# A fused layer norm, autocorrelation and gated FFN on one core: the first group's loads, copies and low parts are put in another order, and the last tile is finished in halves

## Chip, cores, metric
One core of one Trainium2 chip. The metric is the device time of one execution in microseconds (us). TensorE is called PE, VectorE DVE, ScalarE ACT, GpSimd POOL, and the queue of SyncE, which issues most transfers, SP.

## The reference
x is 4096 tokens by 1024. Each token is normalised to xn. A gated feed-forward layer is applied to xn, its weights tiled four times over and with rank-2 additions; its silu is g. s is an autocorrelation of xn: the six strongest lags of each row, softmaxed, weight six rolled copies of xn. The result is x + s*g.

```python
xn = _layernorm(x, axis=-1)
s = _L0_attn_ref(xn)
g = _silu(_L0_ffn_ref(xn, w1q, a1, b1, w3q, a3, b3, w2q, a2, b2))
x = x + s * g
```

The kernel computes on the chip a flag that says whether in every row lag 0 leads by so much that s is xn itself. With these inputs it does, and only the short branch (`dve.Else`) runs.

## The kernel before
The 4096 tokens are worked in 8 groups (`i`) of 512 tokens, each of 4 tiles (`q`) of 128. The quarters of xn are summed first, so that the weights need not be tiled. In a group PE runs:

- **the up stage**, 22 "pairs" (`p`) of hidden columns: `up(i, p)` makes 6 matmuls into a bank of `gb` and 6 into one of `ub` (f16 high and low parts, three products). Every odd pair begins with `lora`, four matmuls of 32 rows that add the rank-2 part from `zst` and `bst` and close the pair before too. ACT's `gate` then writes silu to `sil`, DVE's `product` makes `h`, and `add_chunk` sums four pairs into `acc`, whose high and low parts are `hf_h` and `hf_l`. `bank_free` keeps pair p behind the product of pair p - 3. After p = 5, 9, 13 and 17 comes `z2(i, n)`, eight matmuls of `h` with `a2st`.
- **the down stage**, `down(i, q)`: 34 matmuls of a tile with `w2_h` and `w2_l` into two banks. ACT writes their silu to `gg`, DVE makes `ob` in `multiply` and `add_input`, and SP stores it. The last piece of tile 0 waits for `z2_read`, that is DVE's `z2_stack`. `z_across` ahead of tile 3 waits for `zs`, which DVE's `z_split` writes.

Meanwhile DVE and POOL prepare the next group: `stats` (DVE), `spread` (POOL, small ones), `normalise` (ACT, writes `xn`), `project` (DVE, the 16 dot products of xn with the rows of a1 and a3, tile `junk`), `differences` and `sums` (POOL), `ft_load` and `xt_load` (transposing transfers).

**The first group** has all that is done once beside it. The weights w1 and w3 come in four column blocks (pairs from 0, 4, 10, 16). A block is bounded (`w_bound`, ACT, and `scale_sum` and `w_scale`), scaled and rounded (`w_high`, ACT) and its low part is made (`w_low`, DVE); PE waits for `wl_done` at the first pair of a block. b1 and b3 (tile `raw_b`, ten small transfers) are split by `b_cast` (ACT) and `b_step` (DVE) and scaled by `b_scale` (ACT); PE's `lora` waits for `b_done` at p = 1, 5, 11 and 17. POOL folds tiles 0 and 1, spreads, runs `raw_differences` for four tiles, and copies `a2st` in three pieces, for which the first `z2` waits. The high parts of w2 are ACT's, its six low parts (`w2_low`) POOL's.

The order on each engine is the order of the code; tables of pair numbers say at which pair a step stands. Every wait is a semaphore written out by hand.

```python
if p % 4 == 1 and 4 < p < NP_ - 1:
    z2(i, p // 4 - 1)
...
if n == 0:
    if i:
        pe.wait_ge(z2_read, i)
    else:
        pe.wait_ge(a2_done, 3)
```

Of the kernel before, what the change touches and what calls it, by code (L numbers as in the profile page):

```python
# [95 lines left out]
def build(nc, d):  # L96
# [1284 lines left out]
```

## Time and profile before

| | |
|---|---|
| median of 3 runs | 884.25 us (883.89 to 884.58) |
| the profiled execution | 883.97 us, its span 882.2 us |
| PE busy | 840.8 us (95%) |
| DVE busy | 637.7 us (72%) |
| ACT, POOL busy | 299.7 and 314.1 us |
| first matmul of the up stage of groups 0, 1, 2 | 28.10, 161.88, 263.84 us |
| last matmul starts | 874.93 us |

Times in the trace are from the span's start. A timeline row reads: start, duration, engine, line, operation, tiles, number; in brackets how long the engine had been idle and what ended that. Successive instructions of an engine overlap by a few hundredths of a microsecond, so the distance between two starts is what one costs. Nearly all elementwise operations of ACT are recorded under one line, L550; they are told apart by their tiles.

### The profile page before, as it was taken

Reading aid. Unit: us, or ns where it says so; the run is one execution under the profiler, and the core shown is the slowest. Engines: PE = TensorE matmul, PEld = TensorE weight load, DVE = VectorE, ACT = ScalarE, POOL = GpSimd, SP = SyncE. Lnnn points to the kernel's source line nnn. Section 1 sums busy time; section 2 is a strip of 40 time slices with the busy share of each in tenths; the row PEclk is TensorE's granted clock in tenths of the full one; section 3 lists DMA queues with packets and bytes.
Section 4 is the critical chain, followed back from the end, with each engine's and each line's share of the span. In section 5 each row is a group of like instructions: output and inputs, shape, how many; then the busy total and the mean of one; then the engine's idle time right before and its main releaser. Section 6 shows DMA issues by size and latency. Waiting matters only on the chain.

```text
span 882.2 us, 11146 instructions
## 1 busy us (share of the span) xinstructions
PE 840.8 (95%) x4078; PEld 436.1 (49%) x4078; DVE 637.7 (72%) x979; ACT 299.7 (34%) x448; POOL 314.1 (36%) x405
## 2 busy tenths in 40 slices
PE   5889696999999999999999999999999999999996
PEld 4333255534573346634484436743475345844465
DVE  6878987579767886678866797578866788644534
ACT  4766232332323323233322333233333333122231
POOL 6944754245404344045513444043431465000000
PEclk9899799999999999999999999999999999999999
DMA  9851003411232112501144113321135111320003
GB/s 303 266 169 36 6 25 96 173 31 32 53 126 97 36 30 55 188 28 37 30 116 154 37 31 54 120 96 36 30 55 195 27 32 20 112 96 1 1 2 143
DMA packets 51401, 70.03 MB, mean 79 GB/s; under 512 B 34961, under 2 KB 36849, under 8 KB 51073
## 3 DMA queue, kind: packets, MB, share of 16 engines
q1 hardware_dynamic: 49584, 68.46, 25.2%
q10 hardware_dynamic: 1744, 0.72, 0.3%
q8 instruction: 32, 0.52, 0.3%
q14 instruction: 41, 0.33, 0.1%
HBM read 44.52 MB, written 16.78 MB: 69 GB/s over the span
## 4 chain that ended last, share of the span: by engine, by line
PE 86%; DVE 7%; DVEq 2%; issue 2%; DMA 1%; ACT 1%; SPq 0%; POOL 0%; ACTq 0%
PE g L1123 25%; PE u L1123 23%; PE zb L1213 6%; PE g L1236 5%; PE u L1236 5%; PE u L1243 4%; PE u L1245 4%; PE g L1243 4%; PE g L1245 4%; PE g L1141 3%; DVE junk L769 2%; DMA xf<-in_x 1%; DVEq L830 1%; DVE w_l L989 1%; PE mb L1177 1%
## 5 line engine op out<-in xcount | busy, mean ns | idle before, releaser
L550 ACT ACTIVATE sil<-g,winv 128x512 f32<-128x512 f32 (+1 forms) x176 | 120.2, 684 | 275.3 <-PE g L1141 234.5
L1123 PE MATMUL u<-xt,w_h 128*128 128x512 f16 x672 | 201.4, 382 | 11.2 <-DVE w_l L989 11.2
L1123 PE MATMUL g<-xt,w_h 128*128 128x512 f16 x672 | 203.6, 385 | 1.1 <-DVE w_l L989 0.7
L814 DVE SCALAR_TENSOR_TENSOR h<-u,winv,sil 128x512 f32<-128x512 f32 x168 | 125.6, 748 | 96.6 <-ACT sil L550 82.6
L769 DVE CUSTOM_DVE_ANT_0 junk<-xn,abc 128x1024 bf16<-128x1024 f32 x112 | 159.1, 1421 | 6.7 <-issue 2.4
L438 POOL TENSOR_TENSOR ve<-mv,three 128x1 f32<-128x1 f32 x32 | 7.7, 240 | 355.7 <-DVE mv L751 355.7
L1123 PE MATMUL g<-xt,w_l 128*128 128x512 f16 x336 | 128.6, 383 | 0.0
L1123 PE MATMUL u<-xt,w_l 128*128 128x512 f16 x336 | 128.1, 381 | 0.0
L1123 PEld LDWEIGHTS u<-xt,w_h 128*128 128x128 f16 x672 | 65.9, 98 | 92.7 <-DVE w_l L989 12.7
L1123 PEld LDWEIGHTS g<-xt,w_h 128*128 128x128 f16 x672 | 57.5, 98 | 89.8 <-issue 33.3
L948 DVE SCALAR_TENSOR_TENSOR ob<-xr,c_mean,gg 128x1024 f32<-128x1024 f32 x32 | 41.1, 1284 | 76.9 <-ACT gg L550 52.5
L1236 PE MATMUL g<-w_h,hf_h 128*128 128x512 f32 x192 | 79.9, 416 | 1.4 <-issue 1.0
L1236 PE MATMUL u<-w_h,hf_h 128*128 128x512 f32 x192 | 76.4, 398 | 0.0
L550 ACT ACTIVATE gg<-g 128x512 f32<-128x512 f32 x32 | 19.2, 599 | 158.9 <-PE g L1239 83.8
L1243 PE MATMUL u<-w_l,hf_h 128*128 128x512 f32 x160 | 63.7, 398 | 0.0
L1245 PE MATMUL u<-w_h,hf_l 128*128 128x512 f32 x160 | 63.5, 397 | 0.0
L1243 PE MATMUL g<-w_l,hf_h 128*128 128x512 f32 x160 | 63.2, 395 | 0.0
L1245 PE MATMUL g<-w_h,hf_l 128*128 128x512 f32 x160 | 63.2, 395 | 0.0
L826 DVE TENSOR_TENSOR acc<-acc,h 128x512 f32<-128x512 f32 x80 | 61.7, 771 | 0.0
L1213 PE MATMUL zb<-h,a2st 128*6 128x512 f32 (+1 forms) x352 | 57.5, 593 | 0.0
L1123 PEld LDWEIGHTS g<-xt,w_l 128*128 128x128 f16 x336 | 33.2, 99 | 40.6 <-issue 1.7
L477 POOL TENSOR_TENSOR yh<-xn 128x512 f32<-128x512 f32 x28 | 36.8, 1316 | 45.9 <-ACT xn L550 45.9
(180 smaller groups left out, 1192.3 us busy)
## 6 DMA issues: line engine op xcount, KB each, us to landing
xr<-in_x SPq DMA_DIRECT2D x32, 512.0 KB, 4.6
out_x<-ob SPq DMA_DIRECT2D x32, 512.0 KB, 2.9
xf<-in_x SPq DMA_DIRECT2D x30, 512.0 KB, 3.6
raw_w<-in_w2t SPq DMA_DIRECT2D x1, 2560.0 KB
abc<-in_a SPq DMA_DIRECT2D x1, 2048.0 KB, 10.6
raw_w<-in_w1t SPq DMA_DIRECT2D x2, 768.0 KB, 13.4
raw_w<-in_w3t SPq DMA_DIRECT2D x2, 768.0 KB, 14.7
raw_w<-in_w1t SPq DMA_DIRECT2D x1, 704.0 KB, 15.6
```

What stands on the lines that cost most here:

```text
L477: tt(yh[:], x[:, 0:HALF], x[:, HALF:L], ALU.subtract).then_inc(diff_done, 1)
L550: return nc.scalar.activation(out, in_, f, **kw)
L769: nc.vector.tensor_tensor_reduce(junk[:], xn[:], abc[:, r, :], 1.0, 0.0, ALU.mult, ALU.add, zt[:, q, r:r + 1]).then_inc(z_done, 1)
L814: stt(out=h[0:n, p % NH, :], in0=up, scalar=winv[0:n, 3 * block_of(p) + 1:3 * block_of(p) + 2], in1=sil[0:n, p % 2, :], op0=ALU.mult, op1= ...
L826: o = tt(acc[0:rows, b, :], a, h[0:rows, p % NH, :], ALU.add)
L948: stt(out=o[:], in0=x[:], scalar=c_mean[:, q:q + 1], in1=gg[:], op0=ALU.subtract, op1=ALU.mult)
L1123: o = mm(bank[:], a, x, start=opens and t == 0, stop=closes and t == len(terms) - 1)
L1141: o = mm((gb, ub)[s % 2][k % 3][:], bst[32 * s:32 * s + 32, p // 2, :], zst[32 * s:32 * s + 32, :], start=s >= 2 and not first, stop=s < 2 ...
L1213: o = mm(zb[c:c + 6, :], a2st[0:rows, p, :], h[0:rows, p % NH, :], start=n == 0, stop=p + 4 >= NP_)
L1236: mm(bank[:], hf_h[:, n, t], w2_h[:, n, c:c + 512], start=n == 0, stop=False)
L1243: mm(bank[:], hf_h[:, n, t], w2_l[:, n, c:c + 512], start=False, stop=False)
L1245: mm(bank[:], hf_l[:, n, t], w2_h[:, n, c:c + 512], start=False, stop=False)
```

## The change
- **Loads.** `low` and b's ten transfers are issued by SP behind the four tiles of x, no longer by ACT ahead of its work; `sel` moves behind weight block 1, `abc` ahead of the two next tiles of x.
- **ACT.** A small silu at the very start brings the table in. `w_high(0, 0)` stands ahead of the copies to `xt`, `w_high(1, 0)` ahead of the first gate; b is cast in halves of 5 and 6 pairs of pairs; `b_scale(1)` stands at p = 2, not 3. Bounds and high parts of blocks 2 and 3 stand one or two pairs earlier.
- **DVE.** `w_low(0, 0, *)` stands ahead of `xt_low` and `zc`, low parts of blocks 2 and 3 earlier; six `w2_low` come over from POOL and stand behind the up stage; stats and projections of the first group get other pairs.
- **POOL.** `raw_differences` wait until block 0's four low parts are made (`wl_done`). The fourth stands behind `spread(1, 0)`, and `a2st` behind both.
- **PE.** The spread of z (`mb<-zc,sel`) stands behind the first six matmuls of the up stage; the first group's down stage runs the products with `w2_h` of tiles 0 and 1 first and those with `w2_l` behind.
- **First group's output.** ACT makes rs*g + 1 and adds the mean, DVE is left with one pass a tile.
- **Last tile.** Bank g is finished ahead of bank u, and silu, multiply, add and store run in halves of 512 columns.

```diff
-        STATS_AT = [(2, 8, 14, 19)] + [(1, 7, 13, 19)] * (NG - 1)
-        NORM_AT = [(3, 9, 15)] + [(2, 8, 14, 20)] * (NG - 1)
-        Z_AT = [{(4 if i == 0 else 3) + 6 * q + r: (q, r) for q in range(3) for r in range(4)} for i in range(NG)]
+        STATS_AT = [(3, 11, 17, 19)] + [(1, 7, 13, 19)] * (NG - 1)
+        NORM_AT = [(4, 12, 18)] + [(2, 8, 14, 20)] * (NG - 1)
+        Z_AT = [{p: (n // 4, n % 4) for n, p in enumerate((5, 8, 9, 10, 13, 14, 15, 16, 18, 19, 20, 21))}]
+        Z_AT += [{3 + 6 * q + r: (q, r) for q in range(3) for r in range(4)}] * (NG - 1)
...
-        BOUND_AT = {3: ((2, 0),), 4: ((2, 1),), 5: ((3, 0), (3, 1))}
-        HIGH_AT = {1: ((1, 0), (1, 1)), 6: ((2, 0), (2, 1)), 10: ((3, 0),), 11: ((3, 1),)}
+        BOUND_AT = {2: ((2, 0),), 3: ((2, 1), (3, 0)), 4: ((3, 1),)}
+        HIGH_AT = {1: ((1, 1),), 5: ((2, 0),), 6: ((2, 1),), 8: ((3, 0),), 9: ((3, 1),)}
...
-            for q in FIRST_DIFF:
+            pool.wait_ge(wl_done, 4)
+            for q in FIRST_DIFF[:3]:
                 raw_differences(q)
             pool.wait_ge(zst_done, 1)
-            pool.wait_ge(ab_done, 12)
+            pool.wait_ge(ab_done, 9)
             nc.gpsimd.memset(hf_l[64:P, HN, :].bitcast(F32), 0.0).then_inc(zeroed, 1)
             pool.wait_ge(zeroed, 11)
+            spread(1, 0)
+            raw_differences(FIRST_DIFF[3])
             pool.wait_ge(c_loaded, 16 * 3)
...
             def down(i, q):
-                if i or q:
+                if i == 0 and q:
+                    act.wait_ge(first_mult, q)
+                elif i or q:
                     act.wait_ge(final_done, at_tile(i, q - 1))
...
+                if i == 0:
+                    act.wait_ge(dn_read, 2 * q + 2)
+                    A(gg[:], gg[:], scale=c_rs[:, q:q + 1], bias=1.0).then_inc(plus_done, 1)
+
+            def first_mean(q):
+                act.wait_ge(first_mult, q + 1)
+                A(ob[q % 2][:], ob[q % 2][:], bias=c_mean[:, q:q + 1]).then_inc(final_done, 1)
...
+                if i == 0:
+                    for n in range(1, 3):
+                        w2_low(n)
...
+            def last_output(half):
+                i, q, c = NG - 1, 3, slice(HALF * half, HALF * half + HALF)
...
+                dve.wait_ge(dn_read, at_tile(i, q, 2, half + 1))
+                stt(out=o, in0=x, scalar=c_mean[:, q:q + 1], in1=gg[:, c], op0=ALU.subtract, op1=ALU.mult)
+                drain()
+                stt(out=o, in0=o, scalar=c_rs[:, q:q + 1], in1=x, op0=ALU.mult, op1=ALU.add).then_inc(half_final, 1)
```

Three places as the engines' own orders show them. POOL, from the fourth raw difference (tile `xr_68`) to the first instructions for group 1. Before:

```order
L464 TENSOR_TENSOR yh<-xr_68 128x512 [waits ab_done]
L466 TENSOR_SCALAR yh<-yh,rs 128x512 [waits raw_diff]
L468 TENSOR_TENSOR hl<-yh 128x255 [waits diff_done]
L469 TENSOR_TENSOR hl<-yh 128x255
L470 CAST hl<-yh 128x2
L525 MEMSET hf_l 64x512 [waits ab_done,zst_done]
L529 COPY a2st<-raw_a_116 128x22x2 [waits c_loaded,zeroed]
L529 COPY a2st<-raw_a_116 128x22x2 x2
L438 TENSOR_TENSOR ve<-mv,three 128x1 [waits stats_done]
```

And now:

```order
L540 MEMSET hf_l 64x512 [waits ab_done,zst_done]
L458 TENSOR_TENSOR ve<-mv,three 128x1 [waits stats_done,zeroed]
L459 TENSOR_TENSOR nm<-mv,three 128x1
L461 TENSOR_TENSOR rs<-ve,three 128x1 [waits dev_done]
L463 TENSOR_TENSOR nm<-nm,rs 128x1 [waits dev_done]
L484 TENSOR_TENSOR yh<-xr_68 128x512 [waits ab_done]
L486 TENSOR_SCALAR yh<-yh,rs 128x512 [waits raw_diff]
L488 TENSOR_TENSOR hl<-yh 128x255 [waits diff_done]
L489 TENSOR_TENSOR hl<-yh 128x255
L490 CAST hl<-yh 128x2
L546 COPY a2st<-raw_a_116 128x22x2 [waits c_loaded]
L546 COPY a2st<-raw_a_116 128x22x2 x2
```

The copies to `a2st` now stand behind an instruction that waits for DVE's first `stats` of group 1 (`stats_done`), and behind the fourth difference.

DVE, from the last product of the first group to the first projection of tile 3. Before:

```order
L814 SCALAR_TENSOR_TENSOR h<-g,winv,sil 64x512 [waits z2_done,sil_done]
L847 TENSOR_TENSOR hf_l<-acc,hf_h 128x512 [waits hfh_done]
L835 TENSOR_TENSOR half_a<-half_a,h 64x512 [waits shift_done,zeroed]
L838 TENSOR_TENSOR acc<-half_b,h 32x512 [waits hfl_done,shift_done]
L841 TENSOR_TENSOR acc<-half_b,half_a 32x512 [waits half_done,shift_done]
L847 TENSOR_TENSOR hf_h<-acc,hf_h 64x512 [waits hfh_done]
L1002 SCALAR_TENSOR_TENSOR w_l<-b_hi,low,raw_b_136 64x1024 [waits b2h_done,w2h_done]
L852 SCALAR_TENSOR_TENSOR z2f<-zb,zq 64x512 [waits zq_done]
```

And now:

```order
L830 SCALAR_TENSOR_TENSOR h<-g,winv,sil 64x512 [waits z2_done,sil_done]
L785 ISA junk,zt<-xn,abc 128x1024 [waits z_done]
L785 ISA zt 128x1
L866 TENSOR_TENSOR hf_l<-acc,hf_h 128x512 [waits hfh_done]
L1062 TENSOR_TENSOR w_l<-raw_w_138,w_h 128x1024 [waits w2h_done,zeroed]
L851 TENSOR_TENSOR half_a<-half_a,h 64x512 [waits shift_done]
L854 TENSOR_TENSOR acc<-half_b,h 32x512 [waits hfl_done,shift_done]
L1062 TENSOR_TENSOR w_l<-raw_w_138,w_h 128x1024 [waits w2h_done] x2
L860 TENSOR_TENSOR acc<-half_b,half_a 32x512 [waits half_done,shift_done]
L1062 TENSOR_TENSOR w_l<-raw_w_138,w_h 128x1024 [waits w2h_done]
L866 TENSOR_TENSOR hf_h<-acc,hf_h 64x512 [waits hfh_done]
```

The six low parts of w2 (two more follow) and one projection stand between the last product and `z2f`, which PE's last piece of tile 0 needs.

ACT, from the copy to `bst` for block 0 to the gate of pair 3. Before:

```order
L550 ACTIVATE bst<-bst,wscl 128x256 [waits wscl_done,b_rest_done]
L550 ACTIVATE b_part<-raw_b 128x1152
L550 ACT_TABLE_LOAD
L550 ACTIVATE sil<-g,winv 128x512 [waits g_ready] x2
L550 ACTIVATE w_h<-raw_w_133,wscl 128x2x768 [waits wscl_done] x2
L550 ACTIVATE sil<-g,winv 128x512 [waits mult_done,g_ready]
L550 ACTIVATE b_part<-raw_b 128x1152 [waits b_rest_done]
L550 ACTIVATE sil<-g,winv 128x512 [waits mult_done,g_ready]
L550 ACTIVATE bst<-bst,wscl 128x384 [waits wscl_done,b_rest_done]
```

And now:

```order
L559 ACTIVATE bst<-bst,wscl 128x256 [waits wscl_done,b_rest_done]
L559 ACTIVATE w_h<-raw_w_133,wscl 128x2x768 [waits wscl_done]
L559 ACTIVATE sil<-g,winv 128x512 [waits g_ready] x2
L559 ACTIVATE w_h<-raw_w_133,wscl 128x2x768 [waits wscl_done]
L559 ACTIVATE sil<-g,winv 128x512 [waits mult_done,g_ready]
L559 ACTIVATE bst<-bst,wscl 128x384 [waits wscl_done,b_rest_done]
```

The copy to `bst` for block 1 (128x384), for which PE's pair 5 waits, stands behind the gate of pair 2 with no cast ahead of it.

## Rows read from the trace of the kernel before

**Rows 1.** Windows of the span: part of group 0, then the whole of group 1.

```profile
core 0: us, PE busy (x) PEld busy (x) DVE busy (x) ACT busy (x) POOL busy (x), PEclk, DMA share, GB/s
63.66:122.20 58.54, 48.27 (x238) 19.54 (x235) 51.94 (x76) 25.42 (x38) 30.84 (x32) 0.91 0.09 25
161.88:263.84 101.96, 101.96 (x500) 52.87 (x499) 77.46 (x121) 32.59 (x49) 36.60 (x48) 1.00 0.23 73
```

**Rows 2.** Waits (us, times, longest) of PE in group 0, of DVE from 63.66 to 122.20.

```profile
PE u L1123 <- DVE w_l L989: 11.2, 3, 7.6
DVE h L814 <- ACT sil L550: 5.6, 4, 2.9
```

**Rows 3.** The head: DMA queues of 0 to 60 us, then PE's timeline.

```profile
q10 hardware_dynamic: 1744, 0.72, 4.9%
...
16.22 0.69 PE L1252 MATMUL g<-ident,xf 128*128 128x128 f32 x2 [2.05 <-DMA xf<-in_x]
28.10 1.01 PE L1123 MATMUL g<-xt,w_h 128*128 128x512 f16 x2 [0.65 <-DVE w_l L989]
49.63 0.58 PE L1141 MATMUL g<-zst,bst 32*128 32x512 bf16 x1 [3.48 <-ACT bst L550]
54.11 1.04 PE L1213 MATMUL zb<-h,a2st 128*6 128x512 f32 x8
```

**Rows 4.** Timeline of DVE in the head: low parts of blocks 0 and 1.

```profile
25.24 4.51 DVE L989 SCALAR_TENSOR_TENSOR w_l<-raw_w,wscl,w_h 128x512 f16<-128x512 f32 x4
42.68 1.95 DVE L989 SCALAR_TENSOR_TENSOR w_l<-raw_w,wscl,w_h 128x768 f16<-128x768 f32 x2
```

**Rows 5.** Timeline of POOL: the fourth difference's first and last, copies, spread.

```profile
36.33 1.27 POOL L464 TENSOR_TENSOR yh<-xr 128x512 f32<-128x512 f32 x1
...
41.87 0.19 POOL L470 CAST hl<-yh 128x2 f16<-128x2 f32 x1
42.77 2.10 POOL L529 COPY a2st<-raw_a 128x44 f32<-128x44 f32 x3
46.19 0.19 POOL L438 TENSOR_TENSOR ve<-mv,three 128x1 f32<-128x1 f32 x1 [1.32 <-DVE mv L751]
...
47.13 0.27 POOL L443 TENSOR_TENSOR nm<-nm,rs 128x1 f32<-128x1 f32 x1
```

**Rows 6.** Timelines of DVE and POOL, 81 to 109 us.

```profile
81.28 0.88 DVE L989 SCALAR_TENSOR_TENSOR w_l<-raw_w,wscl,w_h 128x640 f16<-128x640 f32 x1
89.79 2.98 DVE L989 SCALAR_TENSOR_TENSOR w_l<-raw_w,wscl,w_h 128x640 f16<-128x640 f32 x1
92.69 3.35 DVE L769 CUSTOM_DVE_ANT_0 junk<-xn,abc 128x1024 bf16<-128x1024 f32 x1
104.37 1.54 DVE L826 TENSOR_TENSOR acc<-acc,h 128x512 f32<-128x512 f32 x1
108.18 1.21 DVE L769 CUSTOM_DVE_ANT_0 junk<-xn,abc 128x1024 bf16<-128x1024 f32 x1
89.74 5.23 POOL L500 TENSOR_TENSOR w_l<-raw_w,w_h 128x1024 fp32r<-128x1024 f32 x2
```

**Rows 7.** Timelines of DVE and PE behind the up stage, 122 to 153 us.

```profile
124.30 2.86 DVE L835 TENSOR_TENSOR half_a<-half_a,h 64x512 f32<-64x512 f32 x1
130.65 0.68 DVE L841 TENSOR_TENSOR acc<-half_b,half_a 32x512 f32<-32x512 f32 x1 [0.70 <-ACT half_b L550]
132.75 1.28 DVE L1002 SCALAR_TENSOR_TENSOR w_l<-b_hi,low,raw_b 64x1024 fp32r<-64x1024 f32 x1
152.04 1.11 PE L1199 MATMUL mb<-ident,zs 128*128 128x128 f32 x4 [5.60 <-DVE zs L787]
```

**Rows 8.** Timelines of ACT, DVE and SP at the end.

```profile
875.68 0.59 ACT L550 ACTIVATE gg<-u 128x512 f32<-128x512 f32 x1
877.72 1.29 DVE L953 SCALAR_TENSOR_TENSOR ob<-ob,c_rs,xr 128x1024 f32<-128x1024 f32 x1
871.38 8.00 SPq L372 DMA_DIRECT2D out_x<-ob  x2
```

More of the change, by code:

```diff
@@ L370, in store @@
             def store(i, q):
+                if i == NG - 1 and q == 3:
+                    for half in range(2):
+                        c = slice(HALF * half, HALF * half + HALF)
+                        sp.wait_ge(half_final, half + 1)
+                        sp.dma_start(out_d[i * 4 + q][:, c], ob[q % 2][:, c]).then_inc(stored[q % 2], 16)
+                    return
                 sp.wait_ge(final_done, at_tile(i, q))
@@ L531, in _ @@
                 for q in range(4):
-                    if i == 0 and q == 2:
-                        w2_low(0)
-                        w2_low(1)
                     if i + 1 < NG:
-                        spread(i + 1, q)
-                    if i == 0 and q == 2:
-                        w2_low(2)
-                    if i == 0 and q == 3:
-                        for n in range(3, HN + 1):
-                            w2_low(n)
-                    if i + 1 < NG:
+                        if i or q:
+                            spread(i + 1, q)
                         differences(i + 1, q)
@@ L668, in b2_high @@
                 A(b2_hi[64:P, :], raw_b2[64:P, :], ACT.Copy).then_inc(b2h_done, 1)
[L670 to L678 removed]
+            act.wait_ge(zeroed, 4)
+            A(w_sq[:, 0, 0:4], three[:], ACT.Silu).then_inc(table_done, 1)
+            act.wait_ge(table_done, 1)
             w_bound(0, 0)
@@ L702, in _ @@
             b_scale(0)
-            b_cast(1, 0)
+            w_high(1, 0)
             for i in range(NG):
@@ L1038, in _ @@
             x_copy(3)
-            b_step(0, 0)
+            w_low(0, 0, 0)
+            w_low(0, 0, 1)
             xt_low(0)
@@ L1044, in _ @@
             tt(zc[:], zb[:], rsb[:], ALU.mult).then_inc(zc_done, 1)
-            for m in range(2):
-                for k in range(2):
-                    w_low(0, m, k)
-            b_step(0, 1)
+            w_low(0, 1, 0)
+            w_low(0, 1, 1)
+            b_step(0, 0)
             dve.wait_ge(z0_part, 1)
@@ L1223, in down @@
                         pe.wait_ge(dn_read, at_tile(i, 1, 2, 2))
+                if i == NG - 1 and q == 3:
+                    for bank, c in banks:
+                        for n in range(HN):
+                            mm(bank[:], hf_h[:, n, t], w2_h[:, n, c:c + 512], start=n == 0, stop=False)
+                            mm(bank[:], hf_h[:, n, t], w2_l[:, n, c:c + 512], start=False, stop=False)
+                            mm(bank[:], hf_l[:, n, t], w2_h[:, n, c:c + 512], start=False, stop=False)
+                        mm(bank[:], hf_h[:, HN, t], w2_h[:, HN, c:c + 512], start=False, stop=False)
+                        mm(bank[:], hf_l[:, HN, t], w2_l[:, HN, c:c + 512], start=False, stop=True).then_inc(dn_ready, 1)
+                    return
                 for n in ns:
@@ L1276, in z0, with z0_spread @@
                     o.then_inc(z0_ready, 1)
+            def z0_spread():
+                pe.wait_ge(zc_done, 1)
+                pe.wait_ge(sel_loaded, 16)
+                mm(mb[:], sel[:], zc[:], start=True, stop=True).then_inc(z0_ready, 1)
             pe.wait_ge(a_cent, 1)
```

199 lines of the change are left out of this document (142 added, 57 removed).

## The prediction, made before the changed kernel was run
> **What bounds the kernel now.** I read the windows first. Group 1 takes 101.96 us in which PE is busy for 101.96 at the full granted clock, and the groups behind it repeat that [rows 1]. The change leaves them alone, up to the last tile; there is nothing for it to win there. Group 0 runs from 28.1 to 161.88 us [rows 1, 3], 133.8 us, so 31.8 more than its 101.96 of work. With the head ahead of it and the tail behind the last matmul these are the only places where the change acts. PE's waits come next: in group 0 it waits 11.2 us for low parts of w1 and w3 by DVE [rows 2] and 5.6 for `zs`, again DVE's [rows 7]; another 3.5 goes to b's block 1 at pair 5, at 49.63 us [rows 3]. So DVE, or what it waits for, sets group 0. Last I read the engines' timelines at these stalls, to see what each would be late for next.
>
> **The head.** The fourth tile of x lets PE go on at 16.22 us [rows 3]. The queue q10 is b's loads: 4.9% of 16 engines over 60 us, 2.9 us of all of them, which now come behind. I take the 2.9 whole; it is between 0 (they only filled gaps) and about 4. Behind it, DVE's four low parts of block 0 took 4.51 us, 1.13 each, while POOL made differences; block 1's took 0.97 each at 768 columns with POOL elsewhere, 0.65 for 512 [rows 4]. Holding POOL thus saves 1.0 on the two ahead of PE, and `zc`, now behind them, 0.6 by its neighbours. The first matmul of the up stage comes at 28.1 - 2.9 - 1.0 - 0.6 = 23.6 us. The early table load costs nothing: ACT has no input yet. The eleven issues cost SP some 6 us, but in that time the queue works off x and block 0; what moves back (`sel`, blocks 2 and 3) is needed only from 26 us on.
>
> **Pairs 0 to 5.** Part of the 4.5 us goes back: z's spread, its two parts and `zst` now come behind the first six matmuls, and the first gate behind a `w_high` of 1.5 us. Placing each instruction by its duration before, block 1's last low part ends at 42.4 us, against 44.6 (42.68 + 1.95 [rows 4]). The larger step is `b_scale(1)`: it comes with pair 2, near 39 us, so pair 5 starts at 43.7, not at 49.63. With pair 5 and the two scale sums PE is through at 47.3 us, 6.8 ahead of 54.11, where `z2(0, 0)` started [rows 3].
>
> **A wait that replaces the one removed.** `z2(0, 0)` needs `a2st`. Before, POOL had copied it by 44.87 (42.77 + 2.10), long ahead [rows 5]. Now the copies stand behind `spread(1, 0)`, which waits for DVE's first stats of group 1, moved to pair 3 (end 45.2 by my placing), and behind the fourth difference. So: 45.2, spread 1.2 (46.19 to 47.40), difference 5.7 (36.33 to 42.06), copies 2.1 [rows 5] = 54.2, with handovers 54.4. The first three differences, held to 25.4, end near 42 and don't decide. PE stalls 7.1 us, from 47.3 to 54.4: **all that head and pairs 0 to 5 win is gone there.** The difference may cost 5.0 (POOL alone) to 6.8 (the slowest of each kind of its instructions). Behind such a stall PE runs at the lower level, 1.2 GHz, for a while: the mean granted clock of 0.91 over 58.54 us [rows 1] is some 10.5 us at half speed, and PE waited for only 7.6 of them [rows 2], so 3 us of work ran slowly. With 3 to 4 us here I take a loss of 1.9; `z2` ends at 56.3 and pair 6 starts 1.2 us later than before. What is queued behind the waiting PE waits too: ACT and DVE finish pair 5 and then have nothing until `g_ready` of pair 6.
>
> **Pairs 6 to 21: DVE.** From product 7 to product 21 DVE needed 58.54 us [rows 1], 5.6 of them waits for `sil` [rows 2], so 52.9 of work. POOL's low parts of w2 stood in its way there: one low part took 2.98 instead of 0.88, a projection 3.35 instead of 1.21, a sum 1.54 instead of about 0.7 [rows 6], 5.1 in all, and just ahead of PE's 7.6 us wait. Away with them: 47.8. One projection more (1.2), a `b_step` of about 1.0, and less two of block 2's low parts, which come one pair earlier (1.95): 48.1. Product 6 starts at 60.8 (pair 6, partly at the lower level, then `lora` and gate); pair 6's own work is 3.9, and 0.7 is waited at pair 10. Product 21 ends at 60.8 + 3.9 + 48.1 + 0.7 = 113.5, before at 122.2: 8.7 won. Block 3's low parts are there by 86, before PE's pair 16 at 88: its 7.6 wait goes. What is late next is DVE itself, whose products PE trails by `bank_free`.
>
> Here a rule can be weighed. By the row, POOL's 5.23 us of two low parts [rows 6] cost DVE 4.2. The Trainium skill, Perfetto Trace Analysis, Optimizing Scalar/DVE Operations, says that GpSimd and VectorE share an SBUF read port, so that moving work between the two might not help. By that rule this stretch would win nothing; by the rows it wins 5.1 here and pays below.
>
> **From the last product to `zs`.** This took 152.0 - 122.2 = 29.8 us. Added: six `w2_low` at 1.28, the price of DVE's own 1024-column pass at 132.75 [rows 7], 7.7, and a projection, 1.2. Removed: three operations that POOL's low parts stretched, one of them from 0.68 to 2.86 [rows 7], together 5.8; the 0.70 wait ahead of `acc` [rows 7], filled by two low parts; one pass over the tile, 1.4 with its drain; 0.4 that DVE waited for `xn`. The 1.7 that POOL's tile 3 costs stays. Sum 30.4, `zs` at 143.9. Down stage: `z2_read` near 130, and PE, with 18 matmuls of tiles 0 and 1 and 34 of tile 2 left, comes to `z_across` near 143, so the 5.6 wait [rows 7] shrinks to under 1. The later first gate of group 1 (ACT adds 1.2 four times over) has some 2 us to spare before PE's pair 3. Group 1 started 9.84 us behind `z_across` (152.04 [rows 7] to 161.88), 1.3 of it from the lower clock, which falls away: 143.9 + 8.5 = 152.4, **9.5 us earlier**.
>
> **The tail.** Bank g is done 4 us earlier; bank u's silu starts with the last matmul, not 0.5 behind it (875.68 [rows 8]). Multiply and add of 1.29 [rows 8] become 0.68 each, 1.2 less. The last store runs from 879.38 (871.38 + 8.00 [rows 8]) to the end at 882.2; half of it saves between 0 and 0.65, I take 0.4. **2.1 us.**
>
> **Sum.** 883.97 - 9.5 - 2.1 = **872.4 us**, against the profiled execution, which lies 0.3 below the median of 884.25. 0.2% of that, 1.8 us, is what a measurement can tell.
>
> **Rivals.**
> - *The `a2st` wait is short or absent* (stats earlier, differences quicker): then DVE's 7 us without work go, and it reaches product 21 some 6 us earlier: 866. Against it: the order of POOL's instructions. 8%.
> - *Collisions come back.* POOL's tile 3, brought forward, now meets the low parts of w2, and its differences meet DVE in pairs 10 to 18. Two to three hits of 2.2 us, as at 124.30 [rows 7]: 877 to 879. For it: DVE has no slack. 21%.
> - *DVE is freer than that*, the held differences leave it alone and it keeps to PE's pace: 3 to 5 us better, 868. 15%.
> - *The moved work is worth what it costs*, group 0 stays as it was, only the tail wins: 883.97 - 2.1 = 881.9. This is the port rule, as in the Trainium skill's page. 3%.
> - *Slower.* DVE was not late because of POOL's low parts, so only additions remain: 7.7 for six passes in the chain to `zs`, 1.2 for pair 6's later start, less the tail: 883.97 + 7.7 + 1.2 - 2.1 = 890.8. It decides if the relief above (5.1 and 5.8 us) comes to less than 6.8 us. Against it: the stretched operations [rows 6, 7]. 5%.
>
> The forecast's own case has 48% and runs from 869 to 876 (head 0 to 4 is absorbed by the `a2st` wait; difference 5.0 to 6.8; store 0 to 0.65; 2 us for my placing of DVE). The range takes in the faster cases and most of the collisions: 865.5 to 878.5. Faster by over 0.2%: 0.93; within: 0.02; slower: 0.05.
>
> **What would show it.** Right: first matmul of the up stage near 23.6; `z2(0, 0)` waiting about 7 us for POOL's `a2st` and starting near 54.4; no wait at pair 5 or 16; product 21 at 113; `zs` at 144; group 1 at 152; groups at 101.96. Wrong: no wait at `z2(0, 0)`; low parts on DVE well over 1.28 us; group 1 starting outside 149 to 158; a tail from last matmul to end that is not about 5 us.

## The result, and the profile after

| | before | changed |
|---|---|---|
| median | 884.07 us (883.21 to 884.58, 4 runs) | 875.16 us (874.59 to 876.60, 4 runs) |
| ratio | | 0.990, 95% interval 0.9885 to 0.9916 |
| profiled execution | 883.97 us, span 882.2 | 875.03 us, span 873.0 |
| first up matmul of groups 0, 1, 2 | 28.10, 161.88, 263.84 us | 23.00, 154.34, 256.30 us |
| from the last matmul's start to the end | 7.27 us | 5.48 us |

The change is faster by 8.9 us (1%), where 11.6 were forecast (883.97 to 872.4). By the two spans it is 9.2: group 1 starts 7.5 us earlier (forecast 9.5) and again takes 101.96 us [rows 1]; the remaining 1.7 is the tail (forecast 2.1).

Four of PE's waits up to group 1 (us in total, times, longest), where 11.2 us for low parts stood before [rows 2]:

```profile
PE zb L1295 <- POOL a2st L546: 6.5, 1, 6.5
...
PE g L1325 <- DVE hf_l L874: 4.3, 1, 4.3
PE zb L1295 <- DVE h L830: 2.8, 1, 2.8
...
PE u L1203 <- DVE w_l L1049: 2.2, 1, 2.2
```

The forecast's new wait is the longest, and there is none at pair 5 or at pair 16, as forecast. The wait for `hf_l` is the one for `z2_read`: `z2_stack` writes that piece of `hf_l`. PE's timeline at the points of [rows 3, 7] and at group 1's start:

```profile
13.69 0.69 PE L1370 MATMUL g<-ident,xf 128*128 128x128 f32 x2 [2.20 <-DMA xf<-in_x]
...
23.00 0.59 PE L1203 MATMUL g<-xt,w_h 128*128 128x512 f16 x2 [2.74 <-DVE xt L1085]
...
54.15 1.89 PE L1295 MATMUL zb<-h,a2st 128*6 128x512 f32 x8 [6.52 <-POOL a2st L546]
...
131.54 0.77 PE L1325 MATMUL g<-w_h,hf_h 128*128 128x512 f32 x1 [4.35 <-DVE hf_l L874]
132.11 0.63 PE L1325 MATMUL u<-w_h,hf_h 128*128 128x512 f32 x1
132.53 0.63 PE L1327 MATMUL g<-w_l,hf_l 128*128 128x512 f32 x1
...
136.87 0.39 PE L1318 MATMUL u<-w_l,hf_h 128*128 128x512 f32 x1
137.10 0.40 PE L1325 MATMUL g<-w_h,hf_h 128*128 128x512 f32 x1
...
145.97 0.60 PE L1281 MATMUL mb<-ident,zs 128*128 128x128 f32 x4
...
154.34 0.61 PE L1203 MATMUL g<-xt,w_h 128*128 128x512 f16 x2
```

x's fourth tile lands 2.5 us earlier, the first up matmul comes 5.1 earlier, and all of it is gone at 54.15, where `z2(0, 0)` starts as late as before [rows 3]. `z_across`, which had waited 5.60 us for `zs` [rows 7], waits for nothing at 145.97. The rows of 132.11 and 132.53 are new: successive matmuls there start 0.43 us apart; from 136.87 on they start 0.23 apart.

DVE's timeline, and then POOL's, at the same places:

```profile
45.46 0.21 DVE L767 BATCH_NORM_AGGREGATE mv<-bn 128x2 f32<-128x12 f32 x1
...
60.76 0.75 DVE L830 SCALAR_TENSOR_TENSOR h<-u,winv,sil 128x512 f32<-128x512 f32 x1 [7.84 <-ACT sil L559]
...
102.99 1.23 DVE L785 CUSTOM_DVE_ANT_0 junk<-xn,abc 128x1024 bf16<-128x1024 f32 x1 [1.35 <-ACT xn L559]
...
113.79 0.75 DVE L830 SCALAR_TENSOR_TENSOR h<-g,winv,sil 64x512 f32<-64x512 f32 x1
...
123.60 3.45 DVE L1062 TENSOR_TENSOR w_l<-raw_w,w_h 128x1024 fp32r<-128x1024 f32 x2
...
130.13 1.20 DVE L874 SCALAR_TENSOR_TENSOR hf_l<-zh,low,z2f 64x512 fp32r<-64x512 f32 x1 [0.70 <-ACT zh L559]
...
143.70 0.71 DVE L803 CAST zs<-zp 128x64 f32<-128x64 bf16 x6
```

```profile
45.81 0.19 POOL L458 TENSOR_TENSOR ve<-mv,three 128x1 f32<-128x1 f32 x1 [3.36 <-DVE mv L767]
...
47.55 1.27 POOL L484 TENSOR_TENSOR yh<-xr 128x512 f32<-128x512 f32 x1
...
53.57 0.53 POOL L546 COPY a2st<-raw_a 128x44 f32<-128x44 f32 x3
```

Product 6 starts at 60.76, 7.84 us of idle DVE ahead of it. At 102.99, in pair 18, DVE waits 1.35 us for `xn` ahead of a projection. Product 21 starts at 113.79 and ends at 114.54 (before 122.2), `zs` is written by 144.41. In POOL's rows the chain of the new wait stands whole: stats at 45.67, spread to 47.55, fourth difference to 53.57, copies, PE at 54.15.

The tail, DVE's two passes over the second half of the last tile, against 1.29 a pass [rows 8]:

```profile
868.58 0.75 DVE L977 SCALAR_TENSOR_TENSOR ob<-xr,c_mean,gg 128x512 f32<-128x512 f32 x1 [2.23 <-ACT gg L559]
869.41 0.75 DVE L979 SCALAR_TENSOR_TENSOR ob<-ob,c_rs,xr 128x512 f32<-128x512 f32 x1
```

### The profile page after: what moved, and what is told of

It reads as the page before. It is cut to its first block, busy times and chain, and to the rows that moved or that the text cites. A ratio compares the mean times of both kernels' runs of the same rounds, so it can differ in the third digit from the quotient of the medians.

```text
span 873.0 us, 11158 instructions
## 1 busy us (share of the span) xinstructions
PE 836.9 (96%) x4078; PEld 435.7 (50%) x4078; DVE 627.7 (72%) x983; ACT 307.4 (35%) x456; POOL 301.1 (34%) x399
## 4 chain that ended last, share of the span: by engine, by line
PE 88%; DVE 6%; issue 1%; DVEq 1%; POOL 1%; DMA 1%; ACT 1%; SPq 0%; POOLq 0%
PE g L1203 25%; PE u L1203 23%; PE zb L1295 6%; PE g L1354 5%; PE u L1354 5%; PE u L1363 4%; PE u L1361 4%; PE g L1363 4%; PE g L1361 4%; PE g L1221 3%; DMA xf<-in_x 1%; PE mb L1259 1%; DVEq L846 1%; PE u L1357 1%; PE g L1357 1%
## 5 line engine op out<-in xcount | busy, mean ns | idle before, releaser
L785 DVE CUSTOM_DVE_ANT_0 junk<-xn,abc 128x1024 bf16<-128x1024 f32 x112 | 154.8, 1382 | 7.5 <-issue 2.2
L967 DVE SCALAR_TENSOR_TENSOR ob<-xr,c_mean,gg 128x1024 f32<-128x1024 f32 x27 | 34.7, 1284 | 62.1 <-ACT gg L559 41.5
L1354 PE MATMUL g<-w_h,hf_h 128*128 128x512 f32 x174 | 71.9, 413 | 0.0
L1354 PE MATMUL u<-w_h,hf_h 128*128 128x512 f32 x174 | 69.1, 397 | 0.0
L1361 PE MATMUL u<-w_l,hf_h 128*128 128x512 f32 x145 | 57.6, 397 | 0.0
L1363 PE MATMUL u<-w_h,hf_l 128*128 128x512 f32 x145 | 57.6, 397 | 0.0
L1363 PE MATMUL g<-w_h,hf_l 128*128 128x512 f32 x145 | 57.1, 394 | 0.0
L1361 PE MATMUL g<-w_l,hf_h 128*128 128x512 f32 x145 | 57.1, 394 | 0.0
L1203 PEld LDWEIGHTS u<-xt,w_l 128*128 128x128 f16 x336 | 32.9, 98 | 39.8 <-issue 0.3
```

What stands on the lines that cost most here:

```text
L785: nc.vector.tensor_tensor_reduce(junk[:], xn[:], abc[:, r, :], 1.0, 0.0, ALU.mult, ALU.add, zt[:, q, r:r + 1]).then_inc(z_done, 1)
L967: stt(out=o[:], in0=x[:], scalar=c_mean[:, q:q + 1], in1=gg[:], op0=ALU.subtract, op1=ALU.mult)
L1203: o = mm(bank[:], a, x, start=opens and t == 0, stop=closes and t == len(terms) - 1)
L1354: mm(bank[:], hf_h[:, n, t], w2_h[:, n, c:c + 512], start=n == 0, stop=False)
L1361: mm(bank[:], hf_h[:, n, t], w2_l[:, n, c:c + 512], start=False, stop=False)
L1363: mm(bank[:], hf_l[:, n, t], w2_h[:, n, c:c + 512], start=False, stop=False)
```

## The experiments

**How they are read.** All medians stand beside a before of 883.6 to 884.1. Profiled executions of the changed kernel and its variants differ in the head by up to 3.3 us: with the head's code the same, x's fourth tile comes at 12.9 to 14.3 and the first up matmul anywhere from 21.6 to 24.9 (23.0 in the changed kernel's own), and what follows moves with it. So each stretch is read by distances: D1 from the first `z2` to product 21's start, D2 from there to group 1's first matmul.

| | median us (lowest to highest) | first `z2` | product 21 | group 1 | D1 | D2 |
|---|---|---|---|---|---|---|
| before | 884.07 | 54.11 | 121.47 | 161.88 | 67.4 | 40.4 |
| changed | 875.16 (874.6 to 876.6) | 54.15 | 113.79 | 154.34 | 59.6 | 40.6 |
| e1 a2st first | 868.81 (868.4 to 869.2) | 46.62 | 107.03 | 147.77 | 60.4 | 40.7 |
| e2 low parts on POOL | 877.25 (876.2 to 878.1) | 52.24 | 116.94 | 155.60 | 64.7 | 38.7 |
| e3 no hold | 874.66 (872.5 to 876.6) | 51.84 | 111.45 | 152.03 | 59.6 | 40.6 |
| e4 tail whole | 876.34 (875.2 to 880.3) | 56.71 | 116.87 | 157.67 | 60.2 | 40.8 |
| e5 b's loads on ACT | 878.03 (877.4 to 879.5) | 55.50 | 116.04 | 157.02 | 60.5 | 41.0 |
| e6 old output | 876.44 (874.7 to 878.0) | 56.19 | 116.30 | 157.08 | 60.1 | 40.8 |
| e7 e1, tails split | 868.12 (867.5 to 868.6) | 46.12 | 106.70 | 148.03 | 60.6 | 41.3 |
| e8 e7, xn behind z2 | 869.41 (868.3 to 870.0) | 47.68 | 108.09 | 148.75 | 60.4 | 40.7 |
| e9 wait filled | 873.55 (872.9 to 873.9) | 53.39 | 114.16 | 153.31 | 60.8 | 39.2 |
| e10 e1, tile 2 early | 868.99 (866.6 to 872.2) | 47.94 | 108.05 | 148.38 | 60.1 | 40.3 |
| e11 e10, `zs` early | 867.09 (866.9 to 870.8) | 48.68 | 108.89 | 144.35 | 60.2 | 35.5 |
| e12 e1 and e9 | 867.98 (866.1 to 869.9) | 47.68 | 106.90 | 145.87 | 59.2 | 39.0 |

### e1: the copies to a2st ahead of POOL's differences

```diff
+            pool.wait_ge(c_loaded, 16 * 3)
+            for u in range(3):
+                cp(a2st[:, :, 2 * u:2 * u + 2], raw_a2[:]).then_inc(a2_done, 1)
             spread(1, 0)
             raw_differences(FIRST_DIFF[3])
-            pool.wait_ge(c_loaded, 16 * 3)
-            for u in range(3):
-                cp(a2st[:, :, 2 * u:2 * u + 2], raw_a2[:]).then_inc(a2_done, 1)
```

> The changed kernel, with POOL's three copies to a2st moved ahead of the spread of group 1's tile 0 and of the fourth raw difference; nothing else. Theory (PE's 6.5 us wait for a2st empties DVE and ACT, and DVE then sets the rest of the group): the first z2 starts near 47.6 us instead of 54.15 without a wait, DVE's product 6 near 53 instead of 60.76, product 21 ends near 107 instead of 114.5, group 1 starts near 147 instead of 154.34, the time falls from 875.2 to 867 to 869. Rival (PE or DVE merely waits elsewhere, for instance for the four transposes of the raw differences or for more collisions with POOL): the wait is gone but at least half of it comes back before group 1, time 871.5 to 875.

868.81 us, ratio 0.9835 (0.9818 to 0.9851): 6.35 less than the changed kernel. PE's timeline of e1:

```profile
46.62 1.04 PE L1295 MATMUL zb<-h,a2st 128*6 128x512 f32 x8
...
124.79 0.76 PE L1325 MATMUL g<-w_h,hf_h 128*128 128x512 f32 x1 [4.39 <-DVE hf_l L874]
```

No wait at the first `z2`, 7.5 us earlier; product 21 is 6.8 earlier (1.3 of it from this run's quicker head, 21.70 against 23.00). D1 is 0.8 longer, D2 0.1. What the head and pairs 0 to 5 win was lost at this one wait, as the prediction says.

### e2: the six low parts of w2 back on POOL

```diff
+            def w2_low(n):
...
-                    w2_low(4)
-                    w2_low(HN)
```

> The changed kernel with the six low parts of w2 back on POOL, at the places in its order that they had before. Theory (POOL's low parts stretch DVE's operations by more than they save DVE): DVE loses about 5 us in pairs 10 to 21, saves 7.7 behind them and has three stretched operations there again (5.8), so group 1 starts some 3 us later and the time is 877 to 880. Rival (the shared port makes the two places worth the same): 874 to 876. Other rival (DVE is better off without them now that the order is another): 871 to 873.

877.25 us, ratio 0.9932 (0.9916 to 0.9949), 2.1 more than the changed kernel. In this stretch of POOL's timeline, and then of DVE's, the collisions of [rows 6, 7] are back:

```profile
94.00 5.10 POOL L520 TENSOR_TENSOR w_l<-raw_w,w_h 128x1024 fp32r<-128x1024 f32 x2
```

```profile
96.82 3.37 DVE L799 CUSTOM_DVE_ANT_0 junk<-xn,abc 128x1024 bf16<-128x1024 f32 x1
...
119.36 2.87 DVE L865 TENSOR_TENSOR half_a<-half_a,h 64x512 f32<-64x512 f32 x1
122.27 2.78 DVE L868 TENSOR_TENSOR acc<-half_b,h 32x512 f32<-32x512 f32 x1
```

D1 grows from 59.6 to 64.7, 5.1 us; D2 falls from 40.6 to 38.7. The prediction had 5.1 for the first and 1.9 for the second (7.7 less 5.8). The Trainium skill, Perfetto Trace Analysis, Optimizing Scalar/DVE Operations, says only that moving work between GpSimd and VectorE might not help; taken as a rule that nothing is won by it, this case shows otherwise: the sum is some 3 us by the two distances and 2.1 by the medians. On POOL the passes stretched DVE's operations, by 2.16 us (from 1.21 to 3.37) and 2.19 us (from 0.68 to 2.87), each near the 2.55 us of one POOL pass; on DVE they cost their own 1.2 where nothing runs beside them. The Trainium skill, SBUF — State Buffer, SBUF: two separate sides, describes the shared pair as an exclusive lock that is held for a whole instruction; the size of these stretches agrees.

### e3: POOL's differences not held

```diff
-            pool.wait_ge(wl_done, 4)
```

> The changed kernel without POOL's wait for block 0's four low parts ahead of the raw differences. Theory (what decides at pair 5 is DVE's stats of group 1 and the fourth difference behind it, not when the first three begin): the three start near 17.5 instead of 24.9, DVE's low parts of block 0 cost 1.0 instead of 0.65 each, the first up matmul starts 0.7 to 1 us later than 23.0, the first z2 again at 54 to 55, time 874.5 to 876. Rival (the hold is worth its microsecond at the head, or the differences' end decides the z2): 876 to 878, or below 874 if the fourth difference starts earlier.

874.66 us, ratio 0.9907 (0.9890 to 0.9923): the same within the runs, D1 and D2 too. The traces show two effects against each other. On block 0 the hold wins: the two low parts ahead of PE take 1.41 us together in the changed kernel and 1.88 in e3, and the first up matmul comes at 23.00 instead of 23.42, some 0.4 us where the prediction had 1.0. But the held differences then run beside block 1's low parts. DVE's timeline of the changed kernel, then of e3:

```profile
36.20 2.74 DVE L1049 SCALAR_TENSOR_TENSOR w_l<-raw_w,wscl,w_h 128x768 f16<-128x768 f32 x2
40.45 2.25 DVE L1049 SCALAR_TENSOR_TENSOR w_l<-raw_w,wscl,w_h 128x768 f16<-128x768 f32 x2
```

```profile
35.16 1.94 DVE L1048 SCALAR_TENSOR_TENSOR w_l<-raw_w,wscl,w_h 128x768 f16<-128x768 f32 x2
38.43 1.95 DVE L1048 SCALAR_TENSOR_TENSOR w_l<-raw_w,wscl,w_h 128x768 f16<-128x768 f32 x2
```

They cost 1.1 us more there, ahead of the stats from which the `a2st` chain starts. The hold moves the collision and does not remove it. From the first up matmul to the first `z2` e3 needs 28.4 us and the changed kernel 31.2; how much of that the hold costs in the time stays open, since this profile is of e3's fastest run (872.50).

### e4: the last tile whole again

All branches for the last tile's halves are taken out of PE, DVE and SP.

```diff
-                if i == NG - 1 and q == 3:
-                    for half in range(2):
```

> The changed kernel with the last tile whole again: banks alternating, one silu pair, one multiply, one add, one store. Theory: the tail from the last matmul's start to the end goes from 5.5 back to 7.3 us, time 876.8 to 877.2. Rival (halving gains nothing that a run can tell): 875 to 875.5.

876.34 us, ratio 0.9914 (0.9898 to 0.9931). The medians differ by 1.2, less than the theory's 876.8 to 877.2 asks, and two of the four runs (875.23) lie where the rival put them: the time alone does not decide. This profiled execution, 880.28, had a head 2 us late, so its tail alone is read. DVE's timeline of e4:

```profile
872.15 1.28 DVE L961 SCALAR_TENSOR_TENSOR ob<-xr,c_mean,gg 128x1024 f32<-128x1024 f32 x1 [5.29 <-ACT gg L553]
873.51 1.28 DVE L977 SCALAR_TENSOR_TENSOR ob<-ob,c_rs,xr 128x1024 f32<-128x1024 f32 x1
```

From the last matmul's start (870.72) to the end (878.3) it takes 7.6 us, against 5.48 with halves: the halves are worth 2.1 here, 1.8 between before and after. The two passes give 1.0 of that, not 1.2, since a half costs 0.75 to 0.83 and not 0.65.

### e5: b's eleven loads issued by ACT again

```diff
-            sp.dma_start(low[:], d["low"])
...
+            act.dma_start(low[:], d["low"])
```

> The changed kernel with low and b's ten transfers issued by ACT again, ahead of its work and so ahead of most of x. Theory A (what the head wins is swallowed whole by PE's wait for a2st, as the prediction said): the first up matmul comes 2 to 3 us later than 23.0, the first z2 still at 54 to 55, time 875 to 876. Theory B (the a2st chain hangs on DVE's stats of group 1, which stand behind everything DVE does in the head, so a late head makes a late z2): the first z2 starts 2 to 3 us later too, near 57, the wait for a2st is again 6 to 7 us, time 877 to 878.5.

878.03 us, ratio 0.9936 (0.9919 to 0.9953): 2.9 more than the changed kernel. The prediction's own logic, a head that is absorbed by the wait for `a2st`, said nothing would change. PE's timeline of e5, then POOL's:

```profile
55.50 1.89 PE L1295 MATMUL zb<-h,a2st 128*6 128x512 f32 x8 [5.63 <-POOL a2st L537]
```

```profile
47.28 0.19 POOL L449 TENSOR_TENSOR ve<-mv,three 128x1 f32<-128x1 f32 x1 [1.16 <-DVE mv L767]
```

x's fourth tile is 2.0 us later than in the changed kernel's profile (1.4 to 2.8 later than in the ten others with the head's code unchanged), the first up matmul 2.5 (25.52), POOL's spread 1.5 and `z2` 1.35. The absorbing wait does not stand still: its chain begins at DVE's stats of group 1, which stand at pair 3 and are as late as the head. The traces of e4 and e6 show the same with b's loads where the change put them: their first up matmuls are 1.95 and 1.4 us later than the changed kernel's, their `z2` 2.6 and 2.0, and all three wait 6.52 us for `a2st`. Between the two profiles group 1 starts 2.7 us later in e5, half of it already there at `z2`; the medians differ by 2.9. Theory B has the cause and the time right, and the 2 to 3 us at `z2` too large.

### e6: the first group's output in two passes of DVE again

```diff
-                            first_output(q)
+                            multiply(i, q)
+                            add_input(i, q)
```

> The changed kernel with the first group's output as it was: no rs*g + 1 and no mean on ACT, multiply and add on DVE. Theory (zs comes 1.4 us later, but PE reaches z_across only 1.6 us behind zs, so nearly all of it is hidden): 875 to 876. Rival (the second pass stands in the chain that sets group 1): 876.4 to 877.

876.44 us, ratio 0.9907 (0.9885 to 0.9930), its profile with a head 1.4 us later than the changed kernel's. `zs` ends 31.8 us behind product 21's start, against 30.6, but D2 is 40.8 against 40.6: PE comes to `z_across` only then. By these distances the pass that DVE was spared is off the path. The median lies where the rival put it, but the runs go from 874.7 to 878.0 and overlap those of the changed kernel, so the time does not decide.

### e9: PE's wait for z2_read filled with matmuls

This is the test of the term that the prediction lacked. Behind the w2_low products of tile 0 PE runs 18 matmuls into tile 2's banks, whose content is thrown away.

```diff
+                if q == 0:
+                    pe.wait_ge(mult_done, at_pair(0, NP_ - 1))
+                    for n in range(18):
+                        mm((gb, ub)[n % 2][DN[2]][:], hf_h[:, n % HN, t], w2_h[:, n % HN, 0:512], start=True, stop=True)
                 pe.wait_ge(hfl_done, HN + 1)
```

> The changed kernel with 18 matmuls that compute nothing put on PE between the w2_low products of tile 0 and its last products, so that PE's 4.35 us of waiting for z2_read (131.54) are filled with work (18 at 0.23 = 4.2 us) and nothing else changes. Theory (the 17 matmuls behind that wait run at 0.43 instead of 0.23 because PE stood still ahead of them, and this is the term the prediction missed): the last products and tile 1's w2_low products stay at 0.23, PE comes to z_across some 2.0 to 2.3 us after its place less, that is before zs (30.6 us behind product 21), so that a wait of about 0.7 stands there and group 1 starts 39.0 to 39.3 us behind product 21 (now 40.5), 1.3 to 1.6 us less: 873.5 to 874. Rival (they are slow for what runs beside them, DMA at 0.79 and DVE and POOL on SBUF): their spacing stays 0.43 and the time stays 875.

873.55 us, ratio 0.9879 (0.9864 to 0.9894): 1.6 less, by adding work. Windows of the changed kernel and then of e9: the wait, and the 4.9 us behind it (columns as in [rows 1]).

```profile
127.20:131.50 4.30, 0.00 (x0) 0.00 (x0) 3.54 (x4) 0.63 (x1) 4.14 (x5) 0.78 0.15 31
131.50:136.40 4.90, 4.86 (x12) 3.84 (x13) 4.80 (x7) 2.23 (x3) 3.22 (x3) 0.50 0.79 187
```

```profile
127.40:131.90 4.50, 4.50 (x21) 3.60 (x20) 3.71 (x5) 0.63 (x1) 4.34 (x5) 1.00 0.15 29
131.90:136.80 4.90, 4.90 (x23) 3.95 (x22) 4.80 (x7) 2.24 (x3) 3.26 (x3) 1.00 0.81 187
```

With the same DVE, ACT, POOL and DMA load beside it, PE makes 23 matmuls instead of 12 in 4.9 us, and its granted clock is 1.00 (2.4 GHz) instead of 0.50 (1.2 GHz). So what runs beside is not the cause; the empty 4.3 us are. The fill ran 1.05 us too long (to 132.80, while `hf_l` was there at 131.75), hence 1.4 of the 2.3 us in D2.

### e7 and e8: z_split and the low parts in another order

e7 is e1 with `z_split` ahead of `first_output(0)` on DVE, and with the w2_low products of tiles 0 and 1 both ahead of their last products on PE. e8 is e7 with `normalise(1, 3)` behind `z2_copies` again, as before the change, which keeps POOL's tile 3 off DVE's low parts.

```diff
-                    down_low(0)
-                    down_low(1)
+                    down_low_parts(0)
+                    down_low_parts(1)
+                    down_last(0)
+                    down_last(1)
```

> The changed kernel with three things: the copies to a2st first, as in the run before; PE's last pieces of tiles 0 and 1 behind the low products of both tiles, so that 10 more matmuls stand ahead of its wait for z2_read; and z_split ahead of the first output on DVE. Theory (after the a2st wait PE's 4.35 us wait for z2_read and the slow matmuls behind it are what is left, with zs 1.6 us behind as the next bound): the wait for z2_read shrinks by 2.3, zs comes 1.3 earlier, group 1 starts 2 to 2.5 us earlier than with the copies alone (147.77), time 866 to 867. Rival (PE's later work is bound by the banks that ACT empties, one tile after the other): within 0.5 of 868.8.

> The kernel of the run before in this call, with ACT's normalise of tile 3 behind z2's copies again, so that POOL's tile 3 no longer meets DVE's last low parts of w2. Theory: two low parts cost 2.4 instead of 3.45, the last one 1.3 instead of 1.6 and z2_stack 0.7 instead of 1.2, z2_read comes 1.5 to 2 us earlier, but the projections wait 0.3 to 1 us for xn and meet POOL instead; zs within 1 us, time 865 to 867.5. Rival (what DVE saves ahead of z2_read it pays behind it): the same time as the other kernel within 0.5.

e7: 868.12 us, ratio 0.9816 (0.9800 to 0.9833), 0.7 less than e1. Its theory's 866 to 867 is missed. PE's wait for `z2_read` falls from 4.39 to 0.50 us, the matmuls behind it start 0.31 and then 0.23 us apart, and `z_across` comes at 136.18 instead of 139.40 in e1, with 1.63 us of waiting for `zs` ahead of it; but group 1 starts no earlier. PE's timeline, then DVE's:

```profile
138.49 0.79 PE L1360 MATMUL g<-w_h,hf_h 128*128 128x512 f32 x1 [1.65 <-ACT gg L559]
```

```profile
134.17 0.17 DVE L795 CAST zp<-zt 128x16 bf16<-128x16 f32 x1 [3.90 <-issue]
```

Tile 3 waits for ACT to read tile 1's banks, which waits for `first_output(0)`; and ahead of that DVE stands 3.9 us between `some` and its next instruction, which is where the flag is loaded and branched on. e8: 869.41, ratio 0.9831 (0.9815 to 0.9848), no gain. Its six low parts run at 1.2 each without collision and `z2_read` comes 15.6 us behind product 21 instead of 17.6, but xn of tile 3 is then late for the projections, and `some` comes at 22.8 instead of 23.4. The collisions that the changed kernel has behind the up stage are the price of an earlier xn.

### e10 and e11: tile 2 into the wait, zs early, another bank

e10 is e1 with real work in the wait of e9: tile 2's products with w2's high parts (20 of them, not the 24 that the expectation counts). e11 adds `z_split` ahead of `some`, and lets tile 3 use tile 0's banks.

```diff
+                if q == 0:
+                    down_high(2, range(0, HN))
                 pe.wait_ge(hfl_done, HN + 1)
...
+                if i == 0:
+                    z_split()
                 dve.wait_ge(rall_done, i + 1)
...
+                b = 1 if i == 0 and q == 3 else DN[q]
-                        pe.wait_ge(dn_read, at_tile(i, 1, 2, 2))
+                        pe.wait_ge(dn_read, at_tile(i, 1 if i else 0, 2, 2))
```

> On top of e1 (a2st ahead of POOL's differences): tile 2's 24 products with w2's high parts are put between the w2_low products and the last products of tile 0, where PE waits 4.39 us for z2_read, instead of behind tile 1. PE has as much to do, and none of it waits for z2. Theory: the wait at z2_read and the slow stretch behind it go (6.7 us), PE comes to z_across at about 132.8, 24.6 us behind product 21, and there waits 4 to 5 us for zs (29.4 to 30.4 us behind product 21: DVE's chain is not shortened), then runs slowly for 2 us: group 1 starts 39 to 40.5 us behind product 21 (e1: 40.7), 867.5 to 868.8. Rival (PE's own time is what counts): group 1 starts 34 to 35 us behind product 21, 862 to 863.

> On top of e10: DVE's z_split of group 1 is put ahead of the reading of the flag (some, value load and branch, 3.6 us from some to the next instruction), so that zs is there 24.5 to 26 us behind product 21 instead of 30; and group 0's tile 3 is summed in the banks of tile 0, read long before, instead of those of tile 1. Theory (a chain of three: z2_read, then zs, then the bank of tile 1, each hidden behind the one before): with all three gone PE has no wait over 1 us between the last product of the pairs and group 1, and group 1 starts 34 to 36 us behind product 21 (e1: 40.7), 862.5 to 865. Rival (the bank of tile 3 is read too late for group 1's pair 1, or zst, which ACT copies behind two tiles' outputs, comes late): the wait turns up in group 1's pair 1, and the time stays above 866.

e10: 868.99 us, ratio 0.9828 (0.9806 to 0.9851), as e1. e11: 867.09, ratio 0.9809 (0.9795 to 0.9822). PE's timeline of e10, then of e11:

```profile
138.57 1.12 PE L1281 MATMUL mb<-ident,zs 128*128 128x128 f32 x4 [5.03 <-DVE zs L803]
```

```profile
134.63 0.63 PE L1284 MATMUL mb<-ident,zs 128*128 128x128 f32 x4 [0.26 <-DVE some L1165]
144.35 0.59 PE L1206 MATMUL g<-xt,w_h 128*128 128x512 f16 x2 [1.16 <-ACT gg L559]
...
150.07 0.60 PE L1224 MATMUL g<-zst,bst 32*128 32x512 bf16 x1 [2.97 <-ACT gg L559]
151.44 0.63 PE L1206 MATMUL g<-xt,w_l 128*128 128x512 f16 x1
```

In e10 the wait for `z2_read` turned into one for `zs` of 5.03. In e11 that went too, and group 1 starts 35.5 us behind product 21 instead of 40.7, as its theory said; but its pair 1 then waits 2.97 us for the bank in which tile 3 was summed, with matmuls at the lower level behind (0.63 instead of 0.38 for one), as its rival said. Group 2 starts 143.3 us behind product 21 (252.22), against 142.7 in e1 (249.73): by the trace the detour wins nothing, but the trace is that of e11's slowest run (870.84, first up matmul at 24.41 against 21.70 in e1's), and its four other runs, 866.93 to 867.55, lie below all of e1's. Whether e11 wins over e1 stays open.

### e12: e1 and e9 together

> e1 and e9 together: a2st ahead of POOL's differences, and 18 matmuls that compute nothing in PE's wait for z2_read. Theory (the two losses are separate: the a2st wait ahead of product 6, and the slow stretch behind the wait for z2_read): the gains add up, no wait at the first z2, group 1 starts 39.1 us behind product 21 as in e9 (e1: 40.7), 1.5 us less than e1: 867.0 to 867.6. Rival (PE, earlier by 6 us, meets zs or a bank that comes no earlier): 868.5 to 869, like e1.

867.98 us, ratio 0.9823 (0.9807 to 0.9838), between its theory's range and its rival's. D2 is 39.0, as expected for the sum; the median is 0.8 under e1's, with runs from 866.1 to 869.9. That the distances add up is shown, that the time does is not.

## Why the prediction was right, and where it was off

- **Head: right in size, and in part absorbed.** The first up matmul came at 23.00 (forecast 23.6), in a head that varies by 3.3 us from one execution to the next, so that the 0.6 says little. Of the terms, x's fourth tile gave 2.5 (taken: 2.9) and the hold of POOL 0.4 (taken: 1.0, by e3). e5 prices b's loads by themselves: some 2.0 us at x's fourth tile and 2.9 of the median. That the head's gain is "gone there" holds for the profile shown; that it is worth nothing, which the forecast's own range took over ("head 0 to 4 is absorbed"), does not. The stats from which the `a2st` chain starts move with the head.
- **The wait for a2st: right, as a mechanism and as a price.** Forecast 7.1 us ending at 54.4, measured 6.5 ending at 54.15, removed in e1. Within it the terms miss and cancel: stats 0.5 later, spread 1.7 and difference 6.0 instead of 1.2 and 5.7, copies 0.53 instead of 2.10 [rows 5]; that they cancel to 0.3 us is luck. By e3 the late stats are the hold's doing, which the forecast's placing left out: block 1's low parts cost 1.1 more beside the held differences (e3). The stretch at the lower clock behind this wait, taken at 1.9 us of loss, is there: granted clock 0.50 from 54.15 to 57.5, 1.00 from 58.0. The reading on which it rested was off. The forecast took 3 us of slow work behind the 7.6 us wait of the kernel before; its trace has 5.3, matmuls 0.43 us apart from 98.53 to 103.86, since the clock had kept its level for a part of the wait (0.68 in the mean over it).
- **Product 6 at 60.8: right** (60.76). **Product 21's end at 113.5: 1.0 late** (114.54), the stretch from `z2` to it 60.4 instead of 59.1. That POOL's low parts were what held DVE is shown by e2, 5.1 us as priced. The 1.3 is idle time of DVE: between products 6 and 21 it waits 2.0 us (0.35, 0.29 and the 1.35 for `xn` at 102.99) where the forecast had 0.7. The change's tables put the normalising of tile 2 and its first projection both at pair 18; e1, e2, e9 and e10 have the same wait (1.35 or 1.36).
- **zs: right.** 29.9 us behind product 21 instead of 30.4, at 144.41 (forecast 143.9). Its terms cancel too. The collisions that the rival feared are there behind the up stage: two low parts at 3.45 against 2.35 in e8, b's part of `w_l` 1.64 against 1.28, `hf_l` 1.20 against 0.74, four projections 0.9 over 1.21 each, together 2.8 us where the forecast kept 1.7 for POOL's tile 3. Against that the other four low parts cost 1.13 to 1.24 each and not 1.28, and they fill a second wait of 0.70, ahead of the last `hf_h`, that the forecast did not count.
- **The step that failed** is "PE comes to `z_across` near 143, so the 5.6 wait shrinks to under 1", and with it "1.3 of it from the lower clock, which falls away". `z2_read` came at 131.33, not near 130, which is 1.3. And PE, which had stood for 4.35 us for it, ran its next 12 matmuls at 0.43 instead of 0.23: 2.3 us that no term held. I had priced such a stretch behind the wait at 54.4 and not behind this one, which the prediction never named as a wait. So PE reached `z_across` at 145.97, 1.6 behind `zs`; PE, not DVE's `zs`, set the start of group 1. e9 shows the term by itself.
- **Sum.** 0.5 us from `zs`, 1.6 from PE behind it less 0.1 at group 1's start, make 154.34 instead of 152.4; the tail gave 1.7 instead of 2.1 (0.2 of it the passes, by e4).
- **Rivals.** The short `a2st` wait is what e1 makes, not what the change did. The two costs moved (e2) are not equal, and the additions did not decide. The time, 875.16, lies in the forecast's own case, near its upper end; that case had no place for the slow stretch of the step that failed, and that it held the 2 us all the same is partly luck.

All of e1, e7, e8, e10, e11 and e12, which have the copies first, beat both kernels, the slowest of their runs at 872.24 against the changed kernel's fastest at 874.59. e1 is the one to take: three lines moved, no work added, and all its runs between 868.44 and 869.19. e7, e11 and e12 have lower medians by 0.7 to 1.7, at the price of more changes.

## What to carry to other kernels

Where a step is put behind something that it doesn't need, follow from it to who waits: here three copies of 0.5 us in all, placed behind a difference of 6 us and a wait for another engine, took back 6.4 us that the rest of the change had won. Price every wait of PE, a new one and one that was there, with the stretch at the lower clock behind it; a wait that no row shows yet has to be looked for at each `wait_ge` whose producer gets more to do. Follow held work to what it meets next: here the hold took POOL off block 0's low parts and put it on block 1's. And a wait that seems to absorb an earlier gain absorbs it only if its own chain doesn't start from the same place.

## What had not been expected of the hardware

- A stall of PE of 4.35 us was followed by 4.9 us at a granted clock of 0.50; with 18 discarded matmuls in its place the clock stayed at 1.00, and the kernel with more work was the faster (873.55 against 875.16).
- The three copies to `a2st` of 128x44 took 2.10 us beside DVE's low parts of 128x768 in f16 [rows 4, 5], 0.53 in the changed kernel beside an idle DVE, and 0.57 in e1, beside the end of a low part and a product. That the neighbour makes the difference fits these three and was not tried by itself.
- Between reading the flag tile and the next instruction DVE stood 3.6 to 3.9 us in the first group of every kernel here (3.3 to 3.5 in groups 1 and 2 of the changed one), more than any single pass of this stretch. The load of the value is not it: the trace of the changed kernel records it at 0.30 to 0.55 us. By the Trainium skill, Runtime: NRT & Kernel Launch, Instruction fetch mechanics, a taken branch out of the window that is already fetched has to wait for a transfer of its target; no run here shows whether that is what fills the other 3 us.
